# The feed-forward's weights are split in pieces during the attention, and both phases run as one program

## The chip, the cores and the metric

The kernel runs on one core of a Trainium2 chip. The metric is the device time of one execution in microseconds (us). An execution's span goes from its first to its last instruction; its device time is a little longer.

## What is computed

A block of attention and a gated feed-forward, each between two layer norms and with a residual, over 16 sequences of 512 tokens with 512 channels, 32 heads of 16, and 1408 inner channels. All is float32.

```python
def reference(x, Wq, bq, Wk, bk, Wv, bv, Wo, bo, gate_w, up_w, down_w, gate_s, up_s, down_s):
    x = x + _layernorm(attention(_layernorm(x), Wq, bq, Wk, bk, Wv, bv, Wo, bo))
    x = x + _layernorm(ffn(_layernorm(x), gate_w, up_w, down_w, gate_s, up_s, down_s))
    return x
...
def attention(x, ...):                      # causal, with two rotary embeddings on q and k
    q, k, v = x @ Wq.T + bq, x @ Wk.T + bk, x @ Wv.T + bv
    weights = softmax(where(causal, q k^T / sqrt(16), -inf))
    return (weights @ v) @ Wo.T + bo
...
def ffn(x, ...):
    g = einsum('th,ih->ti', x, gate_w) * gate_s
    u = einsum('th,ih->ti', x, up_w) * up_s
    return einsum('ti,hi->th', silu(g) * u, down_w) * down_s
```

## The kernel before

TensorE multiplies float16. So each float32 operand is held as a high and a low half (`w_hi`, `w_lo`, `xT_hi`, `xT_lo`), and a product is a sum of two or three float16 products. A weight matrix is first scaled by a power of two, which needs its largest absolute value over all partitions.

The program is two functions, one after the other, each with SBUF, semaphores and a block of its own. `attention_phase` handles the 16 sequences as a software pipeline written out by hand. `body(i)` exists once on each engine and has NS = 40 steps `s`: eight groups `g` of four heads with five units `u` each. In unit `u` of group `g`:

- TensorE computes the scores for the maxima, ten units ahead (`maxima`), and the transposed scores (`transposed_scores`, into the two banks `ts`, which the exponential of the unit before must have read). In u = 1 it turns the shift (`turn_shift`), in u = 0 and 1 it projects queries or keys, in u = 2 it weighs the values of the group before (`weigh`), in u = 3 and 4 it projects the values or the output (`project_v`, `project_out`).
- VectorE takes the maxima of scores (L753) and the low halves.
- ScalarE takes the exponential in every unit (L587). In u = 2 it first reads the shift (`read_shift`, L593), which frees the bank that `weigh` needs, and adds the bias of queries or keys (`add_bias`); in u = 3 it reads the weighed values (`read_weighed`, L598) into `oT`, of which there is one.
- GpSimd masks, turns for the rotary embedding, averages (`average`, L484) and adds the residual.
- All transfers are issued by SyncE, on one queue, in the order of its own `body`: `place_shift` (L335) puts the shift rows into `qT`, `send_weighed` (L342) writes `oT` out, `fetch_sums`, `send_recips`, `fetch_weighed` (L349 to L364) bring the sums and the weighed values back.

`read_weighed` may not overwrite `oT` before the last write of it has landed:

```python
            def read_weighed(i, g):
                wait_if_any(act, weighed_out, 16 * (NG * i + g))
                act.wait_ge(av_full, NG * i + g + 1)
                nc.scalar.activation(oT[:, :], xb[:, bank_of("av", g), :], ACT.Copy).then_inc(oT_ready, 1)
```

The output projection of sequence i runs one body later, its residual two bodies later; so `body(NB)` and `body(NB + 1)` drain the pipeline. Each engine runs `body(-1)` to `body(NB + 1)`.

`ffn_phase` then loads the first sequence of `x1` and the three weight matrices, 2816 KB each, as float32. `prepare_weights` finds their largest values (L1199), splits them (L1170, L1204, L1208) and sums the low halves to see whether they are all zero (L1175, `rest`, `has_rest`). TensorE then loads `has_rest` into a register and branches to one of two codes: with or without the products of the low halves of the weights. Each of the 16 sequences is a loop pass over NI = 11 blocks (L1342 to L1360); the next sequence is normalised and transposed within it.

## Time and profile before

| | |
|---|---|
| time, three runs | median 2685.45 us (2682.96 to 2690.47) |
| time of the profiled execution | 2681.5 us |
| its span | 2679.8 us |
| busy in the span | TensorE 91%, VectorE 72%, ScalarE 54%, GpSimd 43% |
| attention | from 0 to about 1655 us |
| first matmul of the feed-forward | 1722.8 us |
| mean granted TensorE clock | 0.972 of 2.4 GHz |

The share of busy time is a mean over two very different phases. PE is TensorE's matmuls, PEld its weight loads, DVE is VectorE, ACT is ScalarE, POOL is GpSimd, SPq is SyncE's issue of transfers. A matmul's end is modelled, so a busy PE is not a PE at its peak.

### The profile page before, as it was taken

What the parts mean: (1) busy time and instruction counts of PE and PEld (TensorE: products, weight loads), DVE (VectorE), ACT (ScalarE), POOL (GpSimd) and SP (SyncE); (2) the same over time, 40 slices, a digit from 0 to 9 for tenths busy, and PEclk for the clock granted to TensorE, in tenths of its full rate; (3) what the DMA queues carried; (4) which work ended last, traced back from release to release, by engine and by line L of the source; (5) the groups of instructions that cost most, each with busy time, mean ns of one, the idle gap of its engine ahead of it and who ended that gap; (6) DMA issues with size and microseconds to landing.
All of it is one profiled execution on the core that took longest, in us unless ns stands there. A gap on an engine that the chain in (4) does not pass through costs nothing. (4 is left out here: it accounts for less than half of the span.)

```text
span 2679.8 us, 54601 instructions
## 1 busy us (share of the span) xinstructions
PE 2426.6 (91%) x18816; PEld 1134.6 (42%) x18816; DVE 1931.4 (72%) x5887; ACT 1446.7 (54%) x1902; POOL 1164.6 (43%) x1531
## 2 busy tenths in 40 slices
PE   4889999999999999999999973299999999999997
PEld 2434444444444444444444331144444444444443
DVE  5888889889888888988988853645555555555554
ACT  3577777777777777777777661422222222222221
POOL 3566776777776677677677642000000000000000
PEclk8899999999999999999999987699999999999999
DMA  4444445544554554554454434102111111111111
GB/s 163 120 129 141 159 144 158 168 150 151 167 159 143 166 165 145 159 168 151 143 170 142 142 103 181 72 16 79 47 47 47 63 47 47 73 52 47 47 47 48
DMA packets 178934, 305.62 MB, mean 114 GB/s; under 512 B 32416, under 2 KB 115872, under 8 KB 165536
## 3 DMA queue, kind: packets, MB, share of 16 engines
q1 hardware_dynamic: 178720, 302.86, 34.5%
q8 instruction: 123, 2.02, 0.3%
q14 instruction: 91, 0.75, 0.1%
HBM read 182.73 MB, written 119.01 MB: 113 GB/s over the span
## 5 line engine op out<-in xcount | busy, mean ns | idle before, releaser
L753 DVE CUSTOM_DVE_ANT_0 mx<-mx,causal 128x512 f32<-128x512 f32 (+3 forms) x2048 | 942.6, 517 | 69.7 <-PE mx L864 68.9
L587 ACT ACTIVATE probs<-ts,exp_scale 128x1024 f32<-128x1024 f32 x640 | 710.7, 1111 | 166.8 <-PE ts L878 165.8
L1153 ACT ACTIVATE silu<-gu,gate_scale 128x512 f32<-128x512 f32 x176 | 121.0, 688 | 630.9 <-PE gu L1344 630.9
L1128 POOL TENSOR_TENSOR f_rstd<-f_var,f_neg_half 128x4 f32<-128x4 f32 x32 | 32.3, 1010 | 928.7 <-DVE f_var L1271 646.0
L1294 DVE SCALAR_TENSOR_TENSOR hidden<-gu,up_scale,silu 128x512 f32<-128x512 f32 x176 | 131.9, 749 | 416.6 <-PE gu L1344 406.4
L465 POOL TENSOR_SCALAR_AFFINE_SELECT probs<-probs 128x512 f32<-128x512 f32 x512 | 336.9, 681 | 32.9 <-ACT probs L587 32.7
L892 PE MATMUL xb<-probs,vs 128*32 128x512 f32 (+3 forms) x4096 | 306.4, 440 | 13.4 <-ACT shift_rows L593 12.5
L1342 PE MATMUL gu<-f_xT_hi,gate_hi 128*128 128x512 f16 x704 | 267.7, 380 | 52.5 <-issue 52.5
L878 PE MATMUL ts<-qT,kT 64*128 64x512 f16 (+3 forms) x2048 | 246.0, 298 | 52.9 <-ACT probs L587 50.7
L753 DVE DVE_READ_ACCUMULATOR2_ANT row_max<- 128x1 f32 x2048 | 282.8, 138 | 0.0
L1344 PE MATMUL gu<-f_xT_lo,gate_hi 128*128 128x512 f16 x704 | 267.6, 380 | 0.0
L1356 PE MATMUL down<-down_hi,hid_hi 128*128 128x512 f16 x704 | 266.8, 379 | 0.0
L1342 PE MATMUL gu<-f_xT_hi,up_hi 128*128 128x512 f16 x704 | 266.8, 379 | 0.0
L1344 PE MATMUL gu<-f_xT_lo,up_hi 128*128 128x512 f16 x704 | 266.8, 379 | 0.0
L1360 PE MATMUL down<-down_hi,hid_lo 128*128 128x512 f16 x704 | 266.8, 379 | 0.0
L864 PE MATMUL mx<-kT,qT 64*128 64x512 f16 (+3 forms) x2048 | 252.0, 304 | 8.6 <-DVE row_max L753 7.7
L444 POOL TENSOR_TENSOR turned<-biased,sin_sb 64x512 f32<-64x512 f32 x128 | 163.3, 1276 | 141.8 <-ACT biased L572 135.4
L850 PE MATMUL xb<-xT_hi,w_hi 128*128 128x512 f16 x512 | 199.6, 390 | 11.1 <-issue 9.7
L892 PEld LDWEIGHTS xb<-probs,vs 128*32 128x32 f32 x4096 | 124.8, 110 | 189.8 <-issue 167.7
L850 PE MATMUL xb<-w_hi,xT_hi 128*128 128x128 f16 x1024 | 181.7, 222 | 20.9 <-DVE w_lo L691 11.8
L851 PE MATMUL xb<-xT_lo,w_hi 128*128 128x512 f16 x512 | 197.2, 385 | 0.0
L852 PE MATMUL xb<-xT_hi,w_lo 128*128 128x512 f16 x512 | 196.9, 385 | 0.0
(145 smaller groups left out, 4282.8 us busy)
## 6 DMA issues: line engine op xcount, KB each, us to landing
slots<-half SPq DMA_DIRECT2D x260, 128.0 KB, 13.7
qT<-slots SPq DMA_DIRECT2D x128, 256.0 KB, 3.6
kT<-slots SPq DMA_DIRECT2D x128, 256.0 KB, 3.7
weighed<-oT SPq DMA_DIRECT2D x128, 256.0 KB, 4.5
xn<-x SPq DMA_DIRECT2D x16, 1024.0 KB, 7.4
xr<-x SPq DMA_DIRECT2D x16, 1024.0 KB, 7.8
slots<-half SPq DMA_DIRECT2D x256, 64.0 KB
spread<-recips SPq DMA_DIRECT2D x64, 256.0 KB
```

Of the source, the lines that this page charges most:

```text
L465: nc.gpsimd.affine_select(out=d, in_=d, compare_op=ALU.is_ge, fill=0.0, base=0, pattern=[[0, HG], [1, P]], channel_multiplier=-1).then_inc ...
L587: nc.scalar.activation(probs[:, g % 2, u, :, :], ts[:, :, :], ACT.Exp, scale=exp_scale[:, 0:1]).then_inc(ts_read, 1)
L753: last = nc.vector.tensor_tensor_reduce(out=scores, in0=scores, in1=causal[:, T - P * (qt + 1):T], scale=1.0, scalar=-3e38, op0=ALU.add, o ...
L850: nc.tensor.matmul(out, a_hi, b_hi, start=first, stop=False)
L851: nc.tensor.matmul(out, a_hi, b_lo, start=False, stop=False)
L864: last = nc.tensor.matmul(mx[:, 2 * (n % 2) + j, at:at + P * (qt + 1)], qT[rows, ct, p, P * qt:P * (qt + 1)], kT[rows, ct, p, 0:P * (qt + ...
L878: last = nc.tensor.matmul(ts[:, j, at:at + T - P * kt], kT[rows, ct, p, P * kt:P * (kt + 1)], qT[rows, ct, p, P * kt:T], start=True, stop= ...
L892: last = nc.tensor.matmul(bank[32 * h:32 * h + 32, P * kt:T], vs[:, g // 2, kt, HG * (g % 2) + h, :], probs[:, g % 2, u, j, at:at + T - P ...
L1342: nc.tensor.matmul(gu[:, bank, :], hi[:, c, cols], xT_hi[:, c, :], start=c == 0, stop=False)
L1344: last = nc.tensor.matmul(gu[:, bank, :], hi[:, c, cols], xT_lo[:, c, :], start=False, stop=end and not with_rest)
L1356: nc.tensor.matmul(down[:, t, :], hid_hi[:, b % 3, rows], down_hi[:, b, :], start=b == 0, stop=False)
L1360: last = nc.tensor.matmul(down[:, t, :], hid_lo[:, b % 3, rows], down_hi[:, b, :], start=False, stop=b == NI - 1)
```

## The change

Both phases become one program, `sandwich`, in one block.

- The three weight matrices are handled in NP = 24 pieces of 128x704 elements during the attention, in two passes. In bodies 1 to 6 a piece is loaded every ten steps (`load_piece`) and VectorE takes its largest value (`largest_of_piece`). In body 7 the scales are made. In bodies 8 to 13 each piece is loaded again, ScalarE makes its high half (`high_of_piece`), VectorE its low half (`low_of_piece`), SyncE writes both to a buffer in device memory (`store_piece`, `halves`), and ScalarE sums the low half (`rest_of_piece`).
- In body 15, at step 18, SyncE loads the split halves (`load_ffn_weights`, three transfers of 2816 KB) over the memory of the query, key and value weights, `xn`, `xT`, and other tiles that are no longer read then; all these are now views of one tile `shared`.
- `body(NB)` and `body(NB + 1)` are gone. What is left of them is written out: the last sums, averages and residuals, interleaved with the loading, normalising and transposing of the feed-forward's first sequence. TensorE projects the last output right after that and ahead of the branch; its normalising on ScalarE and its residual on GpSimd fall into the first sequence of the feed-forward.
- `vs` holds 17 columns per head in place of 32, and SyncE's loop over the bodies is unrolled.

```diff
+        PIECE_LOAD, PIECE_MAX, PIECE_HI, PIECE_LO, PIECE_OUT, PIECE_REST = 2, 8, 6, 8, 9, 11
+        def piece_at(i, s, offset, first_body):
+            at = s - offset
+            k, off = divmod(NS * (i - first_body) + at, 2 * NU)
+            return k if off == 0 and 0 <= k < NP else None
...
+            def load_piece(m):
+                n, k = divmod(m % NP, NP // 3)
+                if m < NP:
+                    wait_if_any(sp, piece_max, m)
+                else:
+                    sp.wait_ge(piece_max, NP)
+                    wait_if_any(sp, piece_rest, m - NP)
+                sp.dma_start(raw_piece[:, :], raws[n][:, PIECE * k:PIECE * (k + 1)]).then_inc(piece_in, 16)
+
+            def store_piece(m):
+                n, k = divmod(m, NP // 3)
+                sp.wait_ge(piece_lo, m + 1)
+                sp.dma_start(halves[n, :, :, PIECE * k:PIECE * (k + 1)], split_piece[:, :, :]).then_inc(piece_out, 16)
+
+            def load_ffn_weights():
+                sp.wait_ge(piece_out, 16 * NP)
+                sp.wait_ge(v_full, NC * NB)
+                sp.wait_ge(qk_lo, 8 * NB)
+                sp.wait_ge(slots_out, 64 * 8 * NB)
+                for n in range(3):
+                    sp.dma_start(part(2 * n * G, 2 * G).bitcast(F16).rearrange("p (h e) -> p h e", h=2),
+                                 halves[n]).then_inc(f_weights_in, 16)
...
+                    if i == NB - 1 and s == 18:
+                        load_ffn_weights()
...
+            sp.wait_ge(x1_out, 16)
+            sp.wait_ge(av_full, NG * NB - 1)
+            sp.dma_start(f_xn[:, :, :], x1[0, :, :, :]).then_inc(f_x_in, 16)
+            send_recips(NB - 1, 2)
+            fetch_weighed(NB - 1, 2)
+            send_weighed(NB - 1, NG - 1)
+            fetch_sums(NB - 1, 3)
+            send_recips(NB - 1, 3)
+            fetch_weighed(NB - 1, 3)
...
+            def high_of_piece(m):
+                n = m // (NP // 3)
+                act.wait_ge(f_setup_done, 1)
+                act.wait_ge(piece_in, 16 * (NP + m + 1))
+                wait_if_any(act, piece_out, 16 * m)
+                nc.scalar.activation(split_piece[:, 0, :], raw_piece[:, :], ACT.Copy,
+                                     scale=f_scale[:, n:n + 1]).then_inc(piece_hi, 1)
+
+            def rest_of_piece(m):
+                n, k = divmod(m, NP // 3)
+                act.wait_ge(piece_lo, m + 1)
+                nc.scalar.activation(raw_piece[:, :], split_piece[:, 1, :], ACT.Abs,
+                                     accum_out=rest_pieces[:, n, k:k + 1]).then_inc(piece_rest, 1)
...
+            def largest_of_piece(m):
+                n, k = divmod(m, NP // 3)
+                dve.wait_ge(piece_in, 16 * (m + 1))
+                nc.vector.tensor_reduce(f_largest_pieces[:, n, k:k + 1], raw_piece[:, :], AX.X, ALU.max,
+                                        apply_absolute_value=True).then_inc(piece_max, 1)
...
+            def low_of_piece(m):
+                n = m // (NP // 3)
+                dve.wait_ge(piece_hi, m + 1)
+                nc.vector.scalar_tensor_tensor(split_piece[:, 1, :], raw_piece[:, :], f_scale[:, n:n + 1], split_piece[:, 0, :],
+                                               ALU.mult, ALU.subtract).then_inc(piece_lo, 1)
...
+            bias_of_projected(NB - 2, 3)
+            statistics_of_projected(NB - 2, 3)
+            variance_of_projected(NB - 2)
+            ffn_variance_of_x(0)
+            ffn_normalise_x(0)
+            low_of_attention(NB - 1, 2)
+            reciprocal_of_sums(NB - 1, 3)
+            ffn_low_of_x(0, range(NC))
+            low_of_attention(NB - 1, 3)
+            for t in range(NT):
+                bias_of_projected(NB - 1, t)
+            ffn_sequence(0, False)
...
+            weigh(NB - 1, NG - 1)
+            ffn_transpose_x(0, range(NC))
+            for t in range(NT):
+                for half_of_sum in range(2):
+                    project_out(NB, t, -1, half_of_sum)
+            pe.wait_ge(f_setup_done, 2)
+            pe.wait_ge(f_weights_in, 48)
```

On SyncE, in the second half of body 15 (`shared` is the tile that takes the weights, `halves` the split weights in device memory), before:

```order
L349 DMA sums<-weighed 128x1x32
L335 DMA qT<-shift_rows 4x512 x2
L342 DMA weighed<-oT 128x512
L399 DMA xr<-x 128x2048
L355 DMA recips<-sums 128x32
L335 DMA qT<-shift_rows 4x512 x2
L363 DMA spread<-recips 128x1x512
```

and of the change:

```order
L460 DMA sums<-weighed 128x1x32
L446 DMA qT<-shift_rows 4x512 x2
L498 DMA shared<-halves 128x11264 x3
L453 DMA weighed<-oT 128x512
L543 DMA xr<-x 128x2048
L466 DMA recips<-sums 128x32
L446 DMA qT<-shift_rows 4x512 x2
L474 DMA spread<-recips 128x1x512
```

The three transfers of weights now stand ahead of the write of `oT`, of a shift, and of the return of the sums; the rest keeps its order.

On ScalarE, in the second pass over the pieces, from a unit 1 into unit 2 and on to the next group's unit 1 (`banks` holds all PSUM tiles, `shared` here `biased` or `half`), of the change:

```order
L783 ACTIVATE probs<-banks,exp_scale 128x1024
L761 ACTIVATE projected<-projected,offset,rstd 128x512
L783 ACTIVATE probs<-banks,exp_scale 128x1024
L849 ACTIVATE raw_piece,rest_pieces<-split_piece 128x704
L789 ACTIVATE shift_rows<-banks 8x512
L768 ACTIVATE shared<-banks,bias_qk 128x512
L783 ACTIVATE probs<-banks,exp_scale 128x1024
L794 ACTIVATE oT<-banks 128x512
L783 ACTIVATE probs<-banks,exp_scale 128x1024 x2
L777 ACTIVATE shared<-shared 128x512
L748 ACTIVATE vs<-banks 128x32x16
```

Before, the reading of the shift stood right behind the exponential of unit 1; now a sum over a low half (or, in every other group, the making of a high half, L843) stands between them. The other rows are those of before.

## Rows read from the trace of the kernel before

**Rows 1.** The page: span, and TensorE's busy tenths and clock in 40 slices

```profile
span 2679.8 us, 54601 instructions
PE   4889999999999999999999973299999999999997
```

**Rows 2.** Source view of one SyncE line that runs once per body

```profile
L393 SPq DMA_DIRECT2D xn<-x x15: 348/348/430, 18.0 to 1350.0; - x15
```

**Rows 3.** Windows: stretch, its length, then PE, PEld, DVE, ACT, POOL busy us, clock, DMA share, GB/s

```profile
1350.00:1450.00 100.00, 95.64 (x945) 45.17 (x942) 89.00 (x324) 75.72 (x97) 75.01 (x98) 1.00 0.50 156
1650.00:1700.00 50.00, 3.65 (x16) 3.27 (x16) 34.98 (x29) 11.13 (x6) 3.47 (x7) 0.53 0.63 262
1700.00:1750.00 50.00, 26.94 (x119) 11.70 (x120) 21.23 (x24) 23.90 (x19) 0.37 (x1) 0.75 0.01 1
```

**Rows 4.** Waits from 450 to 1450 us: total us, times, longest us

```profile
DVE roped L735 <- ACT biased L572: 64.2, 58, 2.8
PE xb L892 <- ACT shift_rows L593: 8.7, 12, 0.9
```

**Rows 5.** Timeline, end of the attention: start, us, engine, line, operation, [idle before <- releaser]

```profile
1610.86 2.36 PE L892 MATMUL xb<-probs,vs 128*32 128x512 f32 x32 [0.94 <-DVE projected L762]
...
1630.04 0.61 PE L850 MATMUL xb<-w_hi,aT_hi 128*128 128x512 f16 x1 [14.58 <-DVE aT_lo L728]
...
1641.50 0.38 PE L852 MATMUL xb<-w_hi,aT_lo 128*128 128x512 f16 x1
```

**Rows 6.** The chain that ended last, between the phases: start, us, what

```profile
1655.78 4.79 DMA f_xn<-x
...
1672.09 17.79 DVE f_largest L1199 x3
...
1718.42 4.38 issue
```

**Rows 7.** Timeline: the splitting of the weights, one operation of each kind

```profile
1672.01 6.01 DVE L1199 TENSOR_REDUCE f_largest<-raw_gate 128x1 f32<-128x5632 f32 x1
...
1700.66 6.08 DVE L1208 SCALAR_TENSOR_TENSOR up_lo<-raw_up,f_scale,up_hi 128x5632 f16<-128x5632 f32 x1
1701.03 4.88 ACT L1175 ACTIVATE raw_gate<-gate_lo 128x5632 f32<-128x5632 f16 x1
1705.82 0.19 ACT L1175 ACTIVATION_READ_ACCUMULATOR raw_gate<-gate_lo 128x1 f32 x1
```

**Rows 8.** Transfers: KB each, us from issue to landing

```profile
raw_gate<-gateT SPq DMA_DIRECT2D x1, 2816.0 KB, 11.3
raw_down<-downT SPq DMA_DIRECT2D x1, 2816.0 KB, 23.8
bias_columns_sb<-bias_columns SPq DMA_DIRECT2D x1, 8.0 KB, 12.4
weighed<-oT SPq DMA_DIRECT2D x128, 256.0 KB, 4.5
```

**Rows 9.** Source view of L1104, the feed-forward's load of x1

```profile
DMA to landing us min/median/max: 4.7/4.8/14.2
```

**Rows 10.** Timeline in the middle of body 15

```profile
1562.08 1.31 SPq L335 DMA_DIRECT2D qT<-shift_rows  x2
...
1565.30 0.32 SPq L342 DMA_DIRECT2D weighed<-oT  x1
...
1576.11 0.60 ACT L598 ACTIVATE oT<-xb 128x512 f32<-128x512 f32 x1 [2.82 <-PE xb L892]
```

**Rows 11.** Timeline: unit 1 into unit 2, with an added normalising, and without one

```profile
709.96 0.81 ACT L559 ACTIVATE xn<-xn,offset,rstd 128x512 f32<-128x512 f32 x1
...
711.38 2.36 PE L892 MATMUL xb<-probs,vs 128*32 128x512 f32 x32 [0.86 <-ACT shift_rows L593]
...
721.74 0.57 ACT L593 ACTIVATE shift_rows<-xb 8x512 f16<-8x512 f16 x1
...
722.88 2.36 PE L892 MATMUL xb<-probs,vs 128*32 128x512 f32 x32
```

749 lines of the change are left out of this document (376 added, 373 removed).

## The prediction

> **What bounds the kernel now.** I read the slices of the page first: TensorE is busy nine tenths everywhere except in a hole at slices 25 to 27 of 67 us each, between the two phases [rows 1]. The windows give the engines in each stretch. In the attention (1350 to 1450 us) TensorE is busy 95.6, VectorE 89.0, ScalarE 75.7 and GpSimd 75.0 us of 100; from 1650 to 1700 us TensorE works 3.65 us of 50 [rows 3]. So the hole is nearly pure loss, and the attention is bound by TensorE with VectorE close behind. A body lasts (1350.0 - 18.0)/14 = 95.1 us [rows 2], in which VectorE is idle some 10.5 us. Much of that idle time is VectorE waiting for the bias on ScalarE, 64.2 us in 1000 [rows 4], so it is not free at any place that one likes.
>
> The timeline and the chain show what the hole is made of. The last weighing of values starts at 1610.86; TensorE then stands still for 14.58 us until the last averaged values have come back through device memory; its last output matmul starts at 1641.50 [rows 5]. The feed-forward's first x arrives from 1655.78 on, VectorE looks for the largest weights from 1672.09 for 17.79 us, splits them, and after the branch's register is ready at 1718.42 TensorE needs 4.38 us more [rows 6]. Its first matmul is at 1722.8.
>
> **The change, part by part.**
>
> *The hole.* The largest values, the splits, the sums and the loading of weights leave this place, and so do the residual of sequence 15 and the start of the second program. What stays in front of the feed-forward is the return of the last averaged values and the output projection. Before, the projection ended at 1641.50 + 0.38 = 1641.9. In its way now come the load of the feed-forward's first x (4.8 us to land, rows of the same kind [rows 9]) ahead of the sums of group 6 on SyncE's queue, and VectorE's layer norm and low halves of that x ahead of the last low half. Most of this fits into the 14.58 us of waiting. I take +2 us (from 0, all hidden, to 5, the load's landing in full). The branch costs 4.38 us when nothing is queued; now the last matmuls of the projection are queued in front of it, the last of its four tiles for up to a quarter of the 11.5 us from 1630.04 to 1641.50, 2.9 us [rows 5]. I take 2 us (0 to 4.4). So the feed-forward starts at 1641.9 + 2 + 2 = 1646, against 1722.8: **77 us less**, with bounds of 71 and 81.
>
> By the Trainium skill ("Runtime: NRT & Kernel Launch", section on instruction fetch mechanics) a taken branch whose target is not in the window already fetched has to fetch it before execution can go on. By that rule the 4.38 us of [rows 6] stay whole, and the saving would be 75 us; no row of before shows a branch with work queued ahead of it.
>
> *The load of the split weights.* Three transfers of 2816 KB are issued right after the shift at 1562.08 and ahead of the write of `oT` at 1565.30 [rows 10]. Two rows show that this queue serves in order: 8 KB of bias columns, issued behind 4 MB of weights, took 12.4 us [rows 8], and a load of x that takes 4.8 us took 14.2 us behind the float32 weights [rows 9]. Two of the three weight loads took 23.8 - 11.3 + 2 x 0.47 (the later issues, an estimate from the spacing of such issues) = 13.4 us, 6.7 us each, so three take 20.1 us. Issued at about 1563.4 and with some 2 us until the first bytes count, they land at 1585.5. The write of `oT` behind them (4.5 us alone [rows 8]) lands between 1586 and 1590. ScalarE wanted to overwrite `oT` at 1576.11 [rows 10]: it waits 10 to 14 us, and behind it stand the exponentials, and TensorE behind those. The next shift and the sums stand in the same queue but are due later. With a slow clock after the stop (the matmul after the 14.58 us took 0.61 us, a warm one 0.38 [rows 5]) I take **12 us of new stall**, from 0 (if small transfers pass the large) to 20.
>
> The Trainium skill ("DMA: Bandwidth & Descriptors", section Specifications) gives 358 GB/s as the device memory's limit per core. By that the 8.65 MB would take 24.2 us and the stall would be 16 us. The rows here show 2.88 MB in 6.7 us, 430 GB/s, also from device memory, and the measurement decides.
>
> *The pieces.* A piece has 704 elements, an eighth of 5632. From [rows 7]: the largest value 6.01/8 = 0.75 us, the low half 6.08/8 = 0.76, the sum of a low half 4.88/8 + 0.19 = 0.80; the high half I put at 4.88/8 = 0.61, since it is the same kind of operation on as many elements. A short ScalarE copy of 512 elements takes 0.60 where this scaling gives 0.44 [rows 10], so 0.15 us comes on top on ScalarE and 0.05 on VectorE: 0.80, 0.81, 0.95 and 0.76 us. Times 24: VectorE 19 + 19, ScalarE 23 + 18, together **80 us of added busy time**. What of it is exposed lies between 0 and 80.
>
> First pass, bodies 1 to 6: four times 0.80 us per body on VectorE against 10.5 us idle. VectorE takes the piece in u = 3, past its wait for the bias, and has the next five units to catch up; I expect 0.3 to 0.4 us of each to reach TensorE: 1.5 us per body, 9 us.
>
> Second pass, bodies 8 to 13: the same on VectorE, 1.5 us per body, and eight ScalarE operations in u = 1, each ahead of the reading of the shift. [Rows 11] hold an experiment on this place. Where a normalising of 0.81 us stood there (with others just before), TensorE waited 0.86 us for the shift; in an ordinary group the shift is read by 722.31 and the weighing starts at 722.88, 0.57 us of slack. So 0.76 exposes 0.2, 0.95 exposes 0.4, and where ScalarE is loaded already all of it is exposed: 0.45 us on average. Eight make 3.6 us, 5 with VectorE, 5.3 with the loads and stores in the queue: 32 us in six bodies. For the scales in body 7, some twenty tiny operations in a row on VectorE and a reduction on GpSimd, I allow 3 us. Sum: **44 us of the 80**.
>
> *Nothing else.* 17 columns in place of 32 change the weight loads, which lie beside the fp32 matmuls of `weigh` (2.36 us for 32 [rows 5]); the unrolled loop is SyncE's. I cost both at nothing; if the loads were not covered, the gain would be a few us. The feed-forward's loop is the same; the last normalising and residual of the attention lie beside its TensorE work, as its own `finish` did.
>
> Sum: -77 + 12 + 44 = -21 us on 2681.5 us of the profiled execution, 2660.5. The median of the runs lies 4 us above that execution, so I forecast 2664.
>
> **The rivals.**
>
> *The pieces are hidden.* TensorE is busy 95.6% and bounds the attention; VectorE's 3.2 us per body are less than its 10.5 us of idle time, and ScalarE is idle a quarter. Then pieces cost 5 to 15 us and the time is 2685 - 77 + 12 + 10 = 2630. Against it: TensorE waited for ScalarE at just the place where the pieces go (8.7 us in 1000 [rows 4], 0.86 in one [rows 11]). Chance 0.2.
>
> *The pieces are exposed in full, on both engines (slower).* ScalarE's operation delays the shift, the bias, and with it VectorE's cosine, for which VectorE already waits [rows 4]; VectorE with a piece more has no idle time left to make it good. Then each piece costs its whole time: 80 + 3 + 12 against 77, 18 us slower, 2703. It decides from 65 us, or 1.35 us for each of the 48 places at which pieces are taken. For it speaks that three engines are above 75%; against it that VectorE's first pass alone meets 10.5 us of slack. Chance 0.14.
>
> *The queue.* The load delays not only `oT` but in turn the next sums, their inverse and their return, three trips through device memory of 4.5 us each that SyncE waits for one after the other, and the pieces' loads and stores delay such trips in all bodies. Then the stall is 25 us and the pieces cost 50: 2683, no change. For it: those trips are already what GpSimd waits for. Against: they have slack of several units. Chance 0.14.
>
> **How the numbers follow.** Forecast 0.52 (2645 to 2677, faster), hidden 0.2 (faster), queue 0.14 (2677 to 2693), exposed 0.14 (slower). A change is told from none from about 0.3%, 8 us. Faster 0.72, same 0.14, slower 0.14. The range reaches into both outer cases: 2628 to 2700, which leaves out the lowest of the hidden and the upper half of the exposed case.
>
> **What would show it.** The first feed-forward matmul 77 us nearer to the end of the attention. In body 15, ScalarE's `oT` waiting 10 to 14 us for its own write, once, with slow matmuls behind. The bodies' period: 95 us in body 7 and from 14 on, 1.5 longer in 1 to 6, 5 longer in 8 to 13; TensorE's wait for the shift grown from 8.7 us in 1000 to 30 or more. If the periods of 8 to 13 are 95 to 97 us, or 104 and more, the sum for the pieces is wrong; if `oT` does not wait, the queue is not in order.

## The result: slower by 0.33%, and the profile after

| | before | after |
|---|---|---|
| median (runs) | 2685.45 us (7) | 2695.69 us (7) |
| range of the runs | 2682.96 to 2690.73 | 2689.48 to 2701.11 |
| ratio to before, 95% interval | | 1.0033 (1.0021 to 1.0045) |
| profiled execution, its span | 2681.5, 2679.8 us | 2689.48, 2687.7 us |

The forecast was 2664 us, faster. The time lies inside its range of 2628 to 2700, but the direction was wrong. The profiled execution of the change is the fastest of its seven, 6 us under their median; the account below is of that execution.

The page of the kernel after: the span and TensorE's slices, now of 67.2 us each. They answer to [rows 1].

```profile
span 2687.7 us, 54203 instructions
PE   4889999999988899899899976699999999999997
```

The hole is filled: three slices of 7, 6 and 6 in place of what [rows 1] show. In exchange there are eights where nines stood in the attention, above all in slices 12 to 14 (counted from 1), from 739 to 941 us, where the scales are made. The window in which TensorE worked 3.65 us of 50 [rows 3] now holds 29.66.

**An account by bodies.** ScalarE reads the weighed values into `oT` once per group, eight times per body, so eight such rows later is one body later. From ScalarE's timeline I take the same six of them in both kernels: the 9th, 57th, 65th, 113th, 121st and the 128th, the last. First the kernel before:

```profile
196.94 0.60 ACT L598 ACTIVATE oT<-xb 128x512 f32<-128x512 f32 x1 [1.22 <-PE xb L892]
772.07 0.60 ACT L598 ACTIVATE oT<-xb 128x512 f32<-128x512 f32 x1 [1.23 <-PE xb L892]
867.03 0.60 ACT L598 ACTIVATE oT<-xb 128x512 f32<-128x512 f32 x1 [1.05 <-PE xb L892]
1443.02 0.60 ACT L598 ACTIVATE oT<-xb 128x512 f32<-128x512 f32 x1 [1.19 <-PE xb L892]
1539.17 0.60 ACT L598 ACTIVATE oT<-xb 128x512 f32<-128x512 f32 x1 [1.19 <-PE xb L892]
1613.34 0.60 ACT L598 ACTIVATE oT<-xb 128x512 f32<-128x512 f32 x1 [3.65 <-PE xb L892]
```

And the kernel after:

```profile
195.23 0.60 ACT L794 ACTIVATE oT<-banks 128x512 f32<-128x512 f32 x1 [1.21 <-PE banks L1299]
781.43 0.60 ACT L794 ACTIVATE oT<-banks 128x512 f32<-128x512 f32 x1 [1.04 <-PE banks L1299]
896.00 0.60 ACT L794 ACTIVATE oT<-banks 128x512 f32<-128x512 f32 x1 [1.04 <-PE banks L1299]
1502.15 0.60 ACT L794 ACTIVATE oT<-banks 128x512 f32<-128x512 f32 x1 [1.22 <-PE banks L1299]
1609.14 0.60 ACT L794 ACTIVATE oT<-banks 128x512 f32<-128x512 f32 x1 [1.21 <-PE banks L1299]
1697.19 0.60 ACT L794 ACTIVATE oT<-banks 128x512 f32<-128x512 f32 x1 [3.64 <-PE banks L1299]
```

The differences of neighbouring rows give each stretch. The last is from the last `oT` to the first matmul of the feed-forward, 1722.8 us before [rows 6] and 1731.12 after.

| stretch (us) | before | after | change | forecast |
|---|---|---|---|---|
| start | 196.94 | 195.23 | -1.7 | 0 |
| bodies 1 to 6 (largest values) | 575.1 | 586.2 | +11.1 | +9 |
| body 7 (scales) | 95.0 | 114.6 | +19.6 | +3 |
| bodies 8 to 13 (splits) | 576.0 | 606.2 | +30.2 | +32 |
| body 14 (are there low halves?) | 96.2 | 107.0 | +10.8 | 0 |
| body 15 (load of the halves) | 74.2 | 88.1 | +13.9 | +12 |
| last `oT` to the feed-forward | 109.5 | 33.9 | -75.5 | -77 |

They sum to 8.3 us; the spans differ by 7.9. Five of the seven are within 2.1 us of the forecast. The other two are bodies 7 and 14: 30.4 us where 3 stood. With those 3 the sum would have been some 27 us lower, about 2662.

**What stands in bodies 7 and 14.** GpSimd's timeline of the kernel after, around the reduction over the partitions; the bracket is the idle time ahead of a row and what ended it, "issue" is time in which the engine waited for nothing that the profile shows:

```profile
796.58 1.82 POOL L635 TENSOR_SCALAR_AFFINE_SELECT probs<-probs 128x512 f32<-128x512 f32 x3
806.13 0.39 POOL L685 PARTITION_ALL_REDUCE f_largest_all<-f_largest  x1 [7.74 <-issue]
813.95 0.30 POOL L643 TENSOR_SCALAR shift<-row_max 128x16 f16<-128x16 f32 x1 [7.42 <-issue]
1547.94 0.39 POOL L690 PARTITION_ALL_REDUCE rest_all<-rest  x1 [7.29 <-issue]
1555.47 0.30 POOL L643 TENSOR_SCALAR shift<-row_max 128x16 f16<-128x16 f32 x1 [7.14 <-issue]
```

The operation is shown with 0.39 us, but GpSimd does nothing for 7.74 us ahead of it and for 7.42 behind it. The views of the reduction's line L685 and of the next operation's line L643 show what stands at the start of both stretches, an instruction of GpSimd's sequencer (POOLq; ns: shortest, median, longest, then first and last start in us):

```profile
L685 POOLq MODIFY_POOL_CONFIG  x2: 16/16/16, 798.6 to 798.6; - x2
L643 POOLq MODIFY_POOL_CONFIG  x4: 83/83/83, 806.5 to 1548.3; - x4
```

GpSimd is set up anew at 798.6 for the reduction, which starts 7.5 us later, and back at 806.5 for ordinary operations, the next of which starts 7.4 us later. In the whole trace such rows stand only at the start, and ahead of and behind each reduction. The window from 806 to 815 us of the same execution shows who pays (its length, busy us of TensorE, its weight loads, VectorE, ScalarE and GpSimd, then the granted TensorE clock, DMA share and GB/s):

```profile
806.00:815.00 9.00, 0.08 (x2) 0.11 (x3) 0.00 (x0) 0.00 (x0) 1.36 (x5) 0.50 0.07 24
```

and so do the timelines of TensorE and VectorE right behind it:

```profile
814.92 0.59 PE L1309 MATMUL banks<-ident,shift 128*8 128x128 f16 x4 [14.02 <-POOL shift L648]
819.01 0.75 DVE L982 SCALAR_TENSOR_TENSOR shared<-banks,bias_qk,shared 128x512 f32<-128x512 f32 x1 [13.73 <-ACT shared L768]
```

In these 9 us TensorE works 0.08 and VectorE and ScalarE nothing. TensorE has stood still for 14.02 us, until GpSimd's shift of the next group; the others wait behind it. VectorE's wait is put down to ScalarE's bias; that was late because its matmul was. The granted clock is 0.50 in the window, and the six 512-column matmuls behind the shift take 0.61 to 0.63 us each, where a fast one takes 0.38. Later in body 7 the scales are made in one row of dependent operations on VectorE; of sixteen these are the first and the last:

```profile
856.63 0.64 DVE L64 TENSOR_SCALAR f_power<-f_largest_all 128x3 f32<-128x3 f32 x1
861.28 0.54 DVE L1120 TENSOR_SCALAR down_row<-down_row,f_unscale 128x512 f32<-128x512 f32 x1
```

That is 5.2 us, and the group in which they stand (from one `oT` row to the next) lasts 15.8 us in place of 11.5.

**Body 15 and the hole.** The chain of waits of the kernel after, between 1600 and 1740 us (start, us, what), answers to [rows 5, 6, 10].

```profile
1636.53 22.16 DMA weighed<-oT
1658.72 0.61 ACT oT L794
1659.37 0.61 PE banks L1257
...
1732.59 1.61 issue
```

TensorE's timeline has the first matmul of the feed-forward:

```profile
1731.12 0.39 PE L1411 MATMUL banks<-probs,shared 128*128 128x512 f16 x1 [0.34 <-issue]
```

SyncE issues the write of `oT` at 1636.53, right behind the three loads. It lands 22.16 us later, where it takes 4.5 alone [rows 8]; ScalarE waits for it, and TensorE behind ScalarE. The first matmul after the stop takes 0.61 us, as in [rows 5]. At the branch TensorE is idle for 0.34 us in place of 4.38, with another 1.61 us of issue a few matmuls later: together 1.95, where I had 2. That the 1.61 us belong to the branch is my reading; no run shows it.

TensorE's waits from 890 to 1490 us, by what ended them (us in total, times, longest), after:

```profile
PE banks L1299 <- ACT shift_rows L789: 17.8, 32, 1.6
PE banks L1271 <- DVE row_max L1000: 9.2, 15, 1.4
```

and in the same window before:

```profile
PE xb L892 <- ACT shift_rows L593: 5.0, 6, 0.9
PE mx L864 <- DVE row_max L753: 0.3, 1, 0.3
```

Two waits have grown, one for each engine that got work. Which of them costs the 5.0 us per body needs experiments.

### The profile page after: what moved, and what is told of

The parts are those of the page before. It is cut to its first block, busy times and chain, and to the rows that moved or that the text cites. A ratio compares the mean times of both kernels' runs of the same rounds, so it can differ in the third digit from the quotient of the medians.

```text
span 2687.7 us, 54203 instructions
## 1 busy us (share of the span) xinstructions
PE 2436.7 (91%) x18816; PEld 1125.5 (42%) x18816; DVE 1937.7 (72%) x5930; ACT 1456.4 (54%) x1966; POOL 1174.7 (44%) x1524
## 4 chain that ended last, share of the span: by engine, by line
PE 56%; POOL 13%; issue 12%; DVE 10%; ACT 7%; DMA 2%; SPq 1%; POOLq 0%; DVEq 0%; ACTq 0%
PE banks L1411 11%; PE banks L1413 11%; PE banks L1299 6%; PE banks L1425 5%; PE banks L1429 5%; DVE banks L1000 5%; PE banks L1257 4%; PE banks L1258 3%; PE banks L1259 3%; PE banks L1271 3%; ACT probs L783 2%; POOL shared L616 2%; POOL shared L614 2%; POOL probs L635 2%; PE banks L1285 2%
## 5 line engine op out<-in xcount | busy, mean ns | idle before, releaser
L1000 DVE CUSTOM_DVE_ANT_0 banks<-banks,causal 128x512 f32<-128x512 f32 (+3 forms) x2048 | 942.7, 517 | 73.2 <-PE banks L1271 72.1
L783 ACT ACTIVATE probs<-banks,exp_scale 128x1024 f32<-128x1024 f32 x640 | 710.3, 1110 | 168.9 <-PE banks L1285 168.1
L1411 PE MATMUL banks<-probs,shared 128*128 128x512 f16 x1408 | 533.8, 379 | 2.0 <-issue 2.0
L1413 PE MATMUL banks<-probs,shared 128*128 128x512 f16 x1408 | 533.6, 379 | 0.0
L1257 PE MATMUL banks<-shared 128*128 128x128 f16 (+1 forms) x1536 | 383.0, 279 | 34.5 <-DVE out_lo L938 11.8
L1258 PE MATMUL banks<-shared 128*128 128x128 f16 (+1 forms) x1536 | 379.2, 276 | 0.0
L1259 PE MATMUL banks<-shared 128*128 128x128 f16 (+1 forms) x1536 | 379.2, 276 | 0.0
L1299 PE MATMUL banks<-probs,vs 128*17 128x512 f32 (+3 forms) x4096 | 303.9, 437 | 25.8 <-ACT shift_rows L789 24.8
L1285 PE MATMUL banks<-qT,kT 64*128 64x512 f16 (+3 forms) x2048 | 246.3, 299 | 52.0 <-ACT probs L783 50.1
L1271 PE MATMUL banks<-kT,qT 64*128 64x512 f16 (+3 forms) x2048 | 252.3, 305 | 23.0 <-DVE row_max L1000 21.3
L1425 PE MATMUL banks<-shared,qT 128*128 128x512 f16 x704 | 266.8, 379 | 0.0
L1429 PE MATMUL banks<-shared,qT 128*128 128x512 f16 x704 | 266.8, 379 | 0.0
L614 POOL TENSOR_TENSOR shared<-shared 64x512 f32<-64x512 f32 x128 | 163.3, 1276 | 155.6 <-ACT shared L768 150.0
L1257 PEld LDWEIGHTS banks<-shared 128*128 128x128 f16 x1536 | 150.9, 98 | 162.3 <-issue 94.7
L1411 PEld LDWEIGHTS banks<-probs,shared 128*128 128x128 f16 x1408 | 137.7, 98 | 171.2 <-issue 6.6
L1413 PEld LDWEIGHTS banks<-probs,shared 128*128 128x128 f16 x1408 | 137.8, 98 | 166.0 <-issue 1.9
```

The costliest lines, as they stand in the source:

```text
L783: nc.scalar.activation(probs[:, g % 2, u, :, :], ts[:, :, :], ACT.Exp, scale=exp_scale[:, 0:1]).then_inc(ts_read, 1)
L1000: last = nc.vector.tensor_tensor_reduce(out=scores, in0=scores, in1=causal[:, T - P * (qt + 1):T], scale=1.0, scalar=-3e38, op0=ALU.add, o ...
L1257: nc.tensor.matmul(out, a_hi, b_hi, start=first, stop=False)
L1258: nc.tensor.matmul(out, a_hi, b_lo, start=False, stop=False)
L1259: return nc.tensor.matmul(out, a_lo, b_hi, start=False, stop=last)
L1271: last = nc.tensor.matmul(mx[:, 2 * (n % 2) + j, at:at + P * (qt + 1)], qT[rows, ct, p, P * qt:P * (qt + 1)], kT[rows, ct, p, 0:P * (qt + ...
```

## The experiments

The first four runs, up to the load by ScalarE, were made on one chip, where the kernel before had 2684.39 us. On another (before: 2684.2) ran ScalarE's part behind the shift, the run without the sums, the three parts altered together and the spread scales; on a third (2688.79) the run without the low halves, the transfers alone and the pieces ahead of the cosine; the last run was made on the first chip again (2683.57). A ratio is to the kernel before on the same chip. A time without a ratio is of one execution, so it is good to 5 to 10 us only. "Period" is the mean length of bodies 8 to 13, worked out as above from one profiled execution. To judge small steps: seven traces with the same code in bodies 1 to 6 have 97.0 to 98.2 us per body there, and four with the same code in bodies 8 to 13 have 101.0 to 101.3.

### Two reductions in the kernel before

```diff
+                    if s == 14 and isinstance(i, int) and i in (5, 9):
+                        for k in ((1,) if i == 5 else (2, 3)):
+                            pool.wait_ge(dummy_done, k)
+                            nc.gpsimd.partition_all_reduce(dummy_out[:, :], dummy_in[:, :], P, RMAX).then_inc(dummy_done, 1)
```

> The kernel before, with partition_all_reduces of constants added on GpSimd: one in body 5 and two back to back in body 9, both behind the masks of step 14 and waiting for nothing that is late. Nothing else is changed; their results are not used. Theory A (changing GpSimd to the code of this operation and back is what costs): about 8 us of idle GpSimd ahead of the first reduce and about 7.5 us behind it, so body 5 is 15 to 16 us longer than 95; in body 9 the second of the two follows the first at once, so body 9 is also 15 to 16 us longer, not 31; the time rises by 30 to 32 us. Theory B (the reduce of the changed kernel waited for VectorE's late result, or the place is wrong for it): one costs its 0.4 us, two 0.8, the time rises by 0 to 2 us.

Measured: 2715.78 us, 31.4 more than before. Body 5 lasts 110.4 us in place of 94.9, body 9 with two reductions 111.9 in place of 94.7. GpSimd's timeline of this run:

```profile
604.97 0.39 POOL L520 PARTITION_ALL_REDUCE dummy_out<-dummy_in  x1 [8.71 <-issue]
612.38 0.30 POOL L477 TENSOR_SCALAR shift<-row_max 128x16 f16<-128x16 f32 x1 [7.02 <-issue]
...
1001.86 0.86 POOL L520 PARTITION_ALL_REDUCE dummy_out<-dummy_in  x2 [8.62 <-issue]
1009.71 0.29 POOL L477 TENSOR_SCALAR shift<-row_max 128x16 f16<-128x16 f32 x1 [6.99 <-issue]
```

The data are constants that had long been there, so nothing was waited for. Two in a row cost 17.2 us, one 15.5, and single bodies of the kernel before differ by more than these 1.7 (94.2 to 98.3): the price is not the operation's but that of going over to it, 8.7 us, and of going back to ordinary operations, 7.0 us. `MODIFY_POOL_CONFIG` stands ahead of and behind the pair, and not between the two. In this pipeline nearly all of it reaches the end. This is theory A.

### Both reductions by way of device memory

```diff
+                    if i == SCALES_IN and s == 14:
+                        sp.wait_ge(f_largest_ready, 1)
+                        sp.dma_start(across[:, :], f_largest[:, :]).then_inc(across_out, 16)
+                    if i == SCALES_IN and s == 16:
+                        sp.wait_ge(across_out, 16)
+                        sp.dma_start(raw_piece[:, 0:5 * P], across[:, :].rearrange("(o p) k -> o (p k)", o=1).broadcast_to([P, 5 * P])).then_inc(across_in, 16)
...
-                        nc.gpsimd.partition_all_reduce(f_largest_all[:, 0:5], f_largest[:, 0:5], P, RMAX).then_inc(
+                nc.vector.tensor_reduce(f_largest_all[:, :], raw_piece[:, 0:5 * P].rearrange("q (p k) -> q k p", k=5), AX.X,
+                                        ALU.max).then_inc(f_largest_reduced, 1)
```

> The changed kernel without its two partition_all_reduces in bodies 7 and 14: the 5 (and later 3) values of each partition are written to device memory and read back to every partition as one row, and one VectorE reduction takes the maximum. Theory A: the group that took 27.0 us in body 7 takes 11 to 12, the one that took 25.7 us in body 14 takes 11 to 14; the time falls by 26 to 31 us against the changed kernel, to about 2667 us, 0.7% below the kernel before. Theory B: VectorE's values are just as late, so most of the 16 us and 12 us stay and the time falls by under 8 us. The tiny VectorE operations in body 7 are kept: its group of 15.8 us should stay in either case.

Measured: 2672.3 us, ratio to before 0.9956 (0.9942 to 0.997). Body 7 lasts 100.7 us (114.6 in the changed kernel), body 14 96.3 (107.0): 24.6 us come back. What body 7 still has over its 95.0 lies in the group with the row of scales, 17.7 us, which now also holds VectorE's reduction of 1.32 us. The time fell by 23.4 us, a little less than theory A's 26 to 31, and the group of 15.8 us did not stay as it was. This one edit turns the result round: the changed kernel is then faster than before.

### The load cut in 24 transfers

```diff
-                for n in range(3):
-                    sp.dma_start(part(2 * n * G, 2 * G).bitcast(F16).rearrange("p (h e) -> p h e", h=2),
-                                 halves[n]).then_inc(f_weights_in, 16)
+                    if i == NB - 1 and s >= 18:
+                        for _ in range(2 if s in (20, 30) else 1):
+                            load_ffn_chunk(chunk[0])
+                            chunk[0] += 1
```

> The changed kernel with the load of the split halves in 24 transfers of 352 KB, one at each step from 18 to 39 of body 15 (two at steps 20 and 30), in place of three of 2816 KB at step 18. Theory Q (the write of oT waits its turn behind 20 us of transfers on the same queue): no small transfer has more than one chunk, 0.85 us, in front of it, the 15 us wait of ScalarE for oT is gone and the time falls by 11 to 14 us. Theory W (8.65 MB cost the attention's transfers their bandwidth however they are cut): the stall is spread out but at least 6 us stay.

Measured: 2681.5 us, ratio 0.998 (0.9967 to 0.9992). The seven groups of body 15 last 75.0 us, against 88.1 in the changed kernel and 74.2 before; the median is 14.2 us lower than the changed kernel's. That is theory Q. ScalarE's `oT` is held up by TensorE alone (groups of instructions, 1630 to 1680 us):

```profile
L803 ACT ACTIVATE oT<-banks 128x512 f32<-128x512 f32 x4 | 2.4, 597 | 7.8 <-PE banks L1308 7.8
```

### The load issued by ScalarE, on another queue

```diff
-                    if i == NB - 1 and s == 18:
-                        load_ffn_weights()
...
+                for n in range(3):
+                    act.dma_start(part(2 * n * G, 2 * G).bitcast(F16).rearrange("p (h e) -> p h e", h=2),
+                                  halves[n]).then_inc(f_weights_in, 16)
...
+                    if i == NB - 1 and s == 17:
+                        load_ffn_weights()
```

> The changed kernel with the same three transfers of 2816 KB issued by ScalarE at the end of step 17 of body 15 in place of SyncE at step 18, so that they stand in another queue in front of the same 16 engines. Theory Q: the small transfers of SyncE's queue no longer stand behind them; ScalarE's wait for the landing of oT falls from 15 us to under 5, the weights take longer than 20 us to land, and the time falls by 8 to 13 us. Theory W: the wait stays near 15 us, since as many bytes are in flight at the same time.

Measured: 2683.26 us, in one execution; body 15's groups 84.3 us, only 3.8 us better than with one queue. The time is 12.4 us under the changed kernel's median, inside theory Q's 8 to 13, but only 6.2 under its profiled execution. Six traces with body 15 unaltered have 86.4 to 90.4 us there. ScalarE's wait for the write of `oT` falls from 14.9 to 3.3 us, but the next shift, small as it is, is late (TensorE's waits, 1600 to 1660 us):

```profile
PE banks L1286 <- DMA qT<-shift_rows: 8.7, 2, 6.4
```

So my mechanism, the order of one queue, is only part of it: a small transfer in the other queue is also held up while 8.65 MB are under way. What both have in common is the 16 DMA engines. That these are the cause was not measured by itself; what is shown is that another queue gives back some 4 us of 14 (2 to 6, by those six traces) and short transfers give back 13.

### ScalarE's part of the pieces behind the shift

```diff
-        PIECE_LOAD, PIECE_MAX, PIECE_HI, PIECE_LO, PIECE_OUT, PIECE_REST = 2, 8, 6, 8, 9, 11
+        PIECE_LOAD, PIECE_MAX, PIECE_HI, PIECE_LO, PIECE_OUT, PIECE_REST = 3, 8, 7, 8, 9, 12
```

> The changed kernel with ScalarE's two operations for a piece (high half, sum of the low half) moved from unit 1, ahead of the reading of the shift, to the end of unit 2, behind the reading of the shift and the bias. Nothing is left out. Theory A (what a piece costs in bodies 8 to 13 is mostly its place ahead of the shift, 3.6 of the 5.0 us per body by the prediction): bodies 8 to 13 last 97.5 to 98.5 us in place of 101.0, the whole is 15 to 21 us shorter, 2674 to 2681. Theory B (the work is exposed wherever it stands, since the three busy engines have no room for 1.6 us more per piece): the bodies stay at 100 to 102 us and the time within 5 us of 2695. TensorE's wait for shift rows on ScalarE, 17.8 us in 600, falls to below 8 by A; by B another wait takes its place.

Measured: 2691.86 us, ratio 1.003 (1.0013 to 1.0047); period 101.26 us against 101.03. Theory A, which is the reason that the prediction gave, falls. TensorE's wait for the shift fell from 17.8 to 3.2 us as that theory wanted, but the wait for the exponential rose from 7.9 to 22.2 us. The wait that had grown most in the view was not what set the period.

### Without the sums of the low halves

```diff
-                    m = piece_at(i, s, PIECE_REST, SECOND_PASS)
-                    if m is not None:
-                        rest_of_piece(m)
```

> The changed kernel without ScalarE's sums of the absolute low halves of the pieces: the sums are set to zero, so the search for low halves of the weights that are not zero is left out. It prices one of the two ScalarE operations per piece in bodies 8 to 13, 0.95 us each by the prediction, four per body. Theory A (ahead of the shift the sum exposes 0.4 us or more by itself, with the high half 0.2 and VectorE's part the rest): bodies 8 to 13 last 98.5 to 99.5 us, 2680 to 2687. Theory B (VectorE sets the period of these bodies, the sum is hidden): they stay at 100.5 to 101.5 us and the time at 2692 to 2696. Theory C (all of it is exposed): 97 us, 2671.

Measured: 2689.57 us in one execution, period 101.55 us: theory B by the period (the time is 2.4 us under its 2692 to 2696, as that of the changed kernel's profiled execution is). With VectorE's work in place, ScalarE's sum is free.

### Without the low halves on VectorE, and with the transfers alone

The first takes out `low_of_piece`, the second `high_of_piece` and `rest_of_piece` too. So the first leaves out the low halves of the weights, and the second computes with weights of zero:

```diff
-                    m = piece_at(i, s, PIECE_LO, SECOND_PASS)
-                    if m is not None:
-                        low_of_piece(m)
...
-                    m = piece_at(i, s, PIECE_HI, SECOND_PASS)
-                    if m is not None:
-                        high_of_piece(m)
```

> The changed kernel without VectorE's low halves of the pieces: they are zero, so the weights' low halves are left out; ScalarE's high half and its sum stay where they are, and so do the transfers. In the changed kernel VectorE's operation takes 1.23 us on average in place of the 0.81 predicted (0.94 alone, 1.7 where a GpSimd operation stands beside it), four per body, 4.9 us, as much as the bodies 8 to 13 became longer, 5.0. Theory V (VectorE's low half is what bodies 8 to 13 pay): they last 96 to 97.5 us in place of 101.0, and the time falls by 21 to 30 us, to 2666 to 2675. Theory S (ScalarE's two operations pay, in place or out of place): 99 to 101 us, at most 12 us less. Theory T (the transfers of the pieces delay the sums and weighed values in SyncE's queue): 100 to 101 us.

> The changed kernel with only the transfers of the pieces in bodies 8 to 13: no high half, no low half, no sum; the split weights are zero, so the feed-forward's products are of zeros, at the same number of instructions. Theory T (the transfers pay for themselves in SyncE's queue): bodies 8 to 13 stay above 98 us. Theories V and S: 95.5 to 97 us, and the time 2660 to 2668. Against the run without the low halves alone, it prices ScalarE's share: by V at most 1 us per body, by S 3 or more.

Measured: 2677.5 us, ratio 0.9966 (0.995 to 0.9982), and 2661.25 us in one execution. The 65th and the 113th `oT` row, first without the low halves:

```profile
896.17 0.60 ACT L794 ACTIVATE oT<-banks 128x512 f32<-128x512 f32 x1 [1.04 <-PE banks L1298]
1487.01 0.60 ACT L794 ACTIVATE oT<-banks 128x512 f32<-128x512 f32 x1 [1.04 <-PE banks L1298]
```

and with the transfers alone:

```profile
894.81 0.60 ACT L795 ACTIVATE oT<-banks 128x512 f32<-128x512 f32 x1 [1.16 <-PE banks L1293]
1476.87 0.60 ACT L795 ACTIVATE oT<-banks 128x512 f32<-128x512 f32 x1 [1.04 <-PE banks L1293]
```

Periods (1487.01 - 896.17)/6 = 98.5 and (1476.87 - 894.81)/6 = 97.0 us. With 96.0 before and 101.0 after this is a ladder: transfers 1.0, ScalarE's two operations on top 1.5, VectorE's one operation on top 2.5. No single theory takes it all: V has half, and its expectations of 96 to 97.5 us and of 2666 to 2675 us were too low. The steps hold in this order only, since leaving out ScalarE's sum alone gave nothing. The step of 1.0 is the least sure: it is of the size by which traces of the same code differ in bodies 1 to 6, and it holds whatever else the change did to these bodies (17 columns in place of 32, the unrolled loop).

Why VectorE's share is so large stands in one line of the kernel after, the low halves by themselves (ns: shortest, median, longest):

```profile
L1126 DVE SCALAR_TENSOR_TENSOR split_piece<-raw_piece,f_scale,split_piece x24: 934/1036/2006, 898.4 to 1478.3; 128x704 f16<-128x704 f32 x24
```

The prediction had 0.81 us. Here are one long and one short instance, each with GpSimd's rows beside it:

```profile
898.44 1.68 DVE L1126 SCALAR_TENSOR_TENSOR split_piece<-raw_piece,f_scale,split_piece 128x704 f16<-128x704 f32 x1
898.12 1.27 POOL L616 TENSOR_TENSOR shared<-shared 64x512 f32<-64x512 f32 x1
899.46 1.79 POOL L623 TENSOR_TENSOR shared<-shared 128x512 f32<-128x512 f32 x1
...
973.50 0.95 DVE L1126 SCALAR_TENSOR_TENSOR split_piece<-raw_piece,f_scale,split_piece 128x704 f16<-128x704 f32 x1
972.40 1.27 POOL L616 TENSOR_TENSOR shared<-shared 64x512 f32<-64x512 f32 x1
973.75 1.82 POOL L623 TENSOR_TENSOR shared<-shared 128x512 f32<-128x512 f32 x1
```

At 898.44 GpSimd's turning has 0.95 us to go, and the low half is 0.73 longer than the short one. At 973.50 the turning before has 0.17 us to go, and the next begins 0.25 us into the low half: the low half takes 0.95 us, and it is GpSimd's operation that takes 1.82 in place of 1.27. All 24 instances go this way. In sixteen of them GpSimd's running operation had 0.22 us or more to go, and the low half ended 0.74 to 0.75 us after that operation; in the other eight it took 0.93 to 0.95 us. A GpSimd operation that began within a low half never lengthened it. The mean of the 24 is 1.23 us.

VectorE's low half of the attention's values, which now stands right behind, has a mean of 1.34 us, and 1.06 before. Most of that is not the piece's: in the run without the pieces' low halves it is 1.25 us. So each piece costs VectorE 1.23 us and at most some 0.1 to 0.3 beside it, not 0.8.

The Trainium skill ("SBUF — State Buffer", section on SBUF's two separate sides) says that a VectorE operation with two inputs in SBUF and a GpSimd operation that reads SBUF exclude each other on a shared pair of ports, and that the one that starts first keeps it to its end. The rows above agree: which of the two is longer goes by which of them began first.

### All three mended, scales spread, pieces ahead of the cosine

The first run has the edits of three runs above in one: both reductions by memory, the load in 24 transfers, and ScalarE's part behind the shift. The second spreads the scales in it over 15 steps:

```diff
-                    if i == SCALES_IN and s == 32:
-                        scale_ffn_weights()
+                    if i == SCALES_IN and s >= 23 and s - 23 < 15:
+                        list(scale_steps())[s - 23]()
```

The third has, in place of ScalarE's new order, VectorE's two operations where VectorE stands idle ahead of the cosine:

```diff
+        PIECE_LOAD, PIECE_MAX, PIECE_HI, PIECE_LO, PIECE_OUT, PIECE_REST = 4, 12, 8, 12, 13, 13
...
+                    m = piece_at(i, s, PIECE_LO, SECOND_PASS)
+                    if m is not None:
+                        low_of_piece(m)
                     if u == 2 and exists(i + QUERIES_KEYS[g][1]):
                         cosine(i + QUERIES_KEYS[g][1], QUERIES_KEYS[g][0])
```

> The changed kernel with three parts altered together: both reductions over partitions by way of device memory, the load of the split weights cut into 24 transfers over steps 18 to 39 of body 15, and ScalarE's work on the pieces behind the reading of the shift. Nothing is left out. If the three costs are separate, the gains add: 23 us for the reductions (measured), 14 for the load (measured) and 15 to 20 for the place of the pieces by theory A, so 2640 to 2648; by theory B of the pieces 2655 to 2662. If a gain is given back where another wait ends last, 2665 or more. The kernel before has 2685, so all three readings expect it faster.

> The kernel of the run with three parts altered, and in body 7 the operations that make the scales one per step over steps 23 to 37 in place of all in one row at step 32. Nothing is left out. If the row of some fifteen dependent tiny operations stands in TensorE's way (group 5 of body 7 lasted 15.8 to 17.7 us against 11.5 before), that group comes down to 12 and the time by 4 to 6 us against the run with three parts altered. If each tiny operation costs as much apart as in a row, group 5 falls and groups 6 and 7 grow, and the time stays within 1 us.

> The kernel of the run with three parts altered (2652), with VectorE's two piece operations put ahead of the cosine in unit 2 of groups 0, 2, 4 and 6, where VectorE waits for the bias in groups 2 and 4 (1.5 to 1.6 us) and GpSimd stands still too; ScalarE's high half in unit 3 and its sum in unit 3 of the next group. Nothing is left out. Theory V: in two of four places the operation falls into idle time and costs nothing, and no GpSimd operation stands beside it, 0.94 us each in place of 1.23; bodies 8 to 13 last 98 to 99.5 us in place of 101.5, bodies 1 to 6 some 0.5 to 1 less, together 15 to 24 us less: 2628 to 2640. If the idle time before the cosine isn't free, because the wait is a part of a loop over the engines that every operation lengthens, the time stays within 5 us of 2652.

Measured: 2652.28 us, ratio 0.9883 (0.9859 to 0.9907); 2652.8 us, 0.989 (0.9863 to 0.9917); and 2652.55 us, 0.9865 (0.9841 to 0.9888). The gains of the reductions and of the load add, without a third from ScalarE's order: theory B of the pieces again, 3 us under its 2655 to 2662. Spreading the scales made body 7 2.7 us shorter (96.4 against 99.1), but not the whole, where 4 to 6 us were expected. Nor did the place ahead of the cosine move the time, where 15 to 24 us were expected: by the time, its second reading holds. There the low half has a median of 0.94 us:

```profile
L1144 DVE SCALAR_TENSOR_TENSOR split_piece<-raw_piece,f_scale,split_piece x24: 926/944/1314, 895.7 to 1470.5; 128x704 f16<-128x704 f32 x24
```

but GpSimd does not stand still at all four places: every fourth piece meets it and takes 1.30 us. The period fell from 101.45 us, or 100.8 in the run with spread scales, which has the same code there, to 99.8: 6 to 10 us in six bodies. Bodies 1 to 7 show 6.3 us more than in the run with three parts altered: bodies 1 to 6 last 97.9 us each in place of 97.4, which is within their spread, body 7 102.0 in place of 99.1. So the last run has the pieces ahead of the cosine only in the second pass, and the scales spread:

```diff
-        PIECE_LOAD, PIECE_MAX, PIECE_HI, PIECE_LO, PIECE_OUT, PIECE_REST = 4, 12, 8, 12, 13, 13
+        PIECE_LOAD, PIECE_MAX, PIECE_HI, PIECE_LO, PIECE_OUT, PIECE_REST = 4, 8, 8, 12, 13, 13
```

> The kernel with the pieces ahead of the cosine, but with the first pass's largest values back in unit 3, and with the scales spread one operation per step in body 7. Nothing is left out. In the profiled executions the pieces ahead of the cosine made bodies 8 to 13 some 1.6 us shorter each than in the run with three parts altered (99.8 against 101.45), and spreading the scales made body 7 2.7 us shorter (96.4 against 99.1), yet neither moved the median. If these are real and separate, the sum is 10 + 3 us: 2637 to 2643, ratio to before 0.983 or less. If the periods only move time between stretches, 2648 to 2655, ratio 0.986 to 0.989.

Measured: 2640.57 us (2638.96 to 2641.96), ratio 0.9836 (0.982 to 0.9853), the fastest version here, 1.6% under the kernel before. Its two rows:

```profile
878.22 0.60 ACT L809 ACTIVATE oT<-banks 128x512 f32<-128x512 f32 x1 [1.22 <-PE banks L1333]
1477.88 0.60 ACT L809 ACTIVATE oT<-banks 128x512 f32<-128x512 f32 x1 [1.21 <-PE banks L1333]
```

The time is the one expected, but not by the expected sum. The period is 99.9 us, so bodies 8 to 13 are 9.1 us shorter than in the run with three parts altered and 5.0 shorter than in the one with spread scales. Body 7 lasts 99.7 us here and not 96.4, so what spreading the scales is worth stays open, and with it where the rest of the 12 us between 2652 and 2641 lies.

## Why the prediction was wrong, step by step

- **The scales and the reductions: the step that failed.** "For the scales in body 7, some twenty tiny operations in a row on VectorE and a reduction on GpSimd, I allow 3 us." Measured: 19.6 us in body 7 and 10.8 in body 14, where I had not counted the second reduction at all; together 30.4 us where the sum had 3. With the measured 30.4 in its place, the same sum gives +6 us on the profiled execution, and 7.9 were measured. Some 26 of the 30.4 us are the two reductions (24.6 came back without them, although VectorE then had 1.3 us more to do); the rest is the row of scales. I had read the operation's own 0.4 us. The kernel before has the same two reductions in its hole. This is the first of them in GpSimd's timeline, with the sequencer's rows ahead of it (view of L1132) and behind the second (view of L1128):

```profile
1690.01 0.40 POOL L1132 PARTITION_ALL_REDUCE f_largest_all<-f_largest  x1 [25.16 <-DVE f_largest L1199]
L1132 POOLq MODIFY_POOL_CONFIG  x2: 7/10/12, 1665.1 to 1665.1; - x2
L1128 POOLq MODIFY_POOL_CONFIG  x2: 85/85/85, 1718.2 to 1718.2; - x2
```

  GpSimd goes over to the reduction at 1665.1, 25 us ahead of it, while VectorE still looks for the largest weights, and starts it 0.13 us after VectorE's last result. It goes back at 1718.2, and its next operation is 37 us later. So both steps were paid there in idle time, and the change moved them to where there is none. A third reduction stands at the kernel's start, and GpSimd's timeline shows the idle time around it:

```profile
21.83 0.39 POOL L526 PARTITION_ALL_REDUCE largest_all<-largest  x1 [11.41 <-DVE largest L675]
33.65 1.27 POOL L444 TENSOR_TENSOR turned<-biased,sin_sb 64x512 f32<-64x512 f32 x1 [11.43 <-ACT biased L572]
```

  Both stretches are put down to other engines, and at the start GpSimd had indeed nothing else to do. These rows bound what a reduction costs in a full pipeline by 0.39 us from below and by 11.4 + 0.4 + 11.4 = 23 us from above. An allowance with that upper end, for each of two reductions, would have reached past the time before; I took 3 us and kept no end.
- **The hole** was right: -75.5 for -77. The branch cost less than 4.38 us with work queued ahead of it, as assumed: 0.34 us at the branch and 1.95 with the issue behind it. The Trainium skill ("Runtime: NRT & Kernel Launch", instruction fetch mechanics) has a taken branch fetch its target before execution goes on. The prediction read it so that all 4.38 us would stay; TensorE's idle time did not. Whether the fetch is shorter here or runs beside the queued matmuls, no run shows.
- **The load** was right in size, 13.9 for 12, and the write of `oT` waited 14.9 where I had 10 to 14. The mechanism was half right: another queue gives back only some 4 us.
- **The pieces** were right in sum, 41.3 for 41, and wrong in their parts. For bodies 8 to 13 I had 1.5 us per body for VectorE, 3.6 for ScalarE ahead of the shift, 0.2 for the transfers; the ladder gives 2.5, 1.5 and 1.0. "0.76 exposes 0.2, 0.95 exposes 0.4" came from one place in the trace, and moving ScalarE's operations away from it changed nothing. The low half's price of 0.81 us was scaled from [rows 7], from a stretch in which GpSimd stood still; in the pipeline it takes 0.94 us when it need not wait for GpSimd, and 1.23 in the mean. That the sum came out is luck: two errors cancelled.
- **Bodies 1 to 6** were right: 11.1 for 9. With 97.0 to 98.2 us per body in seven traces, 3 us either way mean nothing here.
- **The rivals.** The one that ended on the slower side had the pieces exposed in full; it is not what happened, and the slower result does not speak for it. "Hidden" is refuted by the period of 101.0. No rival had the reductions: their cost was nowhere in the range as a mechanism, only as luck of its width.

## What to carry to other kernels

Before an operation moves from a stretch where its engine is idle into a full pipeline, look at the idle time on both sides of it where it stands: a stretch that is put down to another engine can hide a cost of its own, and the duration in the trace says nothing of it. Here the rows of the engine's sequencer gave it away: a `MODIFY_POOL_CONFIG` long ahead of the reduction. Scale a duration only from a stretch in which the same neighbours are at work. When the cause is a wait at one place, moving the work away and leaving it out are the two tests: here the wait vanished from the view and the time did not move.

## What the runs showed of the hardware

- A reduction over partitions on GpSimd between ordinary operations cost 7.3 to 8.7 us ahead and 7.0 to 7.4 us behind, each of the four times; two in a row paid once. Each of these stretches begins with a `MODIFY_POOL_CONFIG` row. Where GpSimd had to wait for other engines anyway, as in the hole of the kernel before, they cost nothing. The Trainium skill ("GPSIMD Engine Reference", section on instruction dispatch) states an invisible load of code of some 6 us at the first call of a freshly loaded routine. The runs agree in kind, show more, and show a second one on the way back, which came as a surprise. That it is code that is loaded, no row here shows.
- 8.65 MB in three transfers delay a write of 256 KB in the same queue from 4.5 to 22.16 us, and shift rows of 4 KB in another queue by up to 6.4 us. In 24 transfers of 352 KB between the others they cost 0.8 us (75.0 against 74.2).
- A VectorE operation that reads two operands of 704 elements from SBUF took 0.94 us alone. Begun while a GpSimd operation ran, it ended 0.75 us after that one and took up to 2.0 us; a GpSimd operation begun within it went from 1.27 to 1.79 us or more. The one that began first was not lengthened by the other.
